# Reordering the tile body of a fused two-layer kernel on TensorE, ScalarE and VectorE

## The reference

```python
x = x + tanh(g_xattn[0]) * attention(layernorm(x), mask, ctx)         # 32 heads of 8, plus adapter attention
x = x + tanh(g_ffn[0]) * top1_experts(layernorm(x))                   # 8 experts 256x256
x = x + tanh(g_xattn[1]) * wkv(w, u, layernorm(x), ctx)               # a decaying scan over 64 steps
x = x + tanh(g_ffn[1]) * top2_experts(layernorm(x))                   # 8 gated experts, integer softmax
```

## Time and profile before

| | us |
|---|---|
| three executions | 501.67, 503.9, 503.55 |
| median | 503.55 |
| the profiled execution | 506.51 |
| its span in the trace | 504.1 |
| PE busy in the span | 464.0 (92%) |
| PE weight loads busy | 356.0 (71%) |
| DVE busy | 383.5 (76%) |
| ACT busy | 260.6 (52%) |
| POOL busy | 178.0 (35%) |

### The profile page before, as it was taken

How to read it: one execution, slowest core, us unless ns; L and a number is a source line. 1 busy time by engine, 2 the same in 40 slices (tenths; PEclk the granted TensorE clock), 3 DMA queues, 4 the chain that set the end, 5 groups by cost and what they waited for, 6 DMA issues and landing times. The chain is left out here.

```text
span 504.1 us, 10504 instructions
## 1 busy us (share of the span) xinstructions
PE 464.0 (92%) x3147; PEld 356.0 (71%) x3148; DVE 383.5 (76%) x1015; ACT 260.6 (52%) x564; POOL 178.0 (35%) x228
## 2 busy tenths in 40 slices
PE   4979899899998998999989898999999999999993
PEld 2748677777787787886866654555778788788782
DVE  5865879898889998999877889957776576575640
ACT  2755284473663752845712352525557657666641
POOL 4234212224124124231141061214455566665522
PEclk9979999899899998999999999999999999999998
DMA  7940404004004021040040589548667667668611
GB/s 225 285 93 17 74 1 85 7 23 85 16 12 86 25 53 36 21 83 18 13 85 26 197 308 383 167 138 276 237 167 248 206 208 258 187 225 235 179 22 21
DMA packets 24785, 63.37 MB, mean 126 GB/s; under 512 B 5192, under 2 KB 15312, under 8 KB 21808
## 3 DMA queue, kind: packets, MB, share of 16 engines
q1 hardware_dynamic: 19472, 56.38, 36.9%
q0 software_dynamic: 4416, 6.03, 6.5%
q10 hardware_dynamic: 864, 0.54, 0.3%
HBM read 48.79 MB, written 5.24 MB: 107 GB/s over the span
## 5 line engine op out<-in xcount | busy, mean ns | idle before, releaser
L2070 PE MATMUL bank_o<-w,hT 128*128 (+1 forms) x276 | 68.3, 389 | 2.0 <-DVE hT L1419 1.0
L1433 DVE TENSOR_TENSOR wl<-lw,wh 128x1024 fp32r<-128x1024 f32 (+1 forms) x54 | 60.9, 1129 | 1.4 <-ACT wh L652 1.4
L2070 PEld LDWEIGHTS bank_o<-w,hT 128*128 128x128 f32 (+1 forms) x276 | 48.8, 189 | 16.2 <-issue 11.5
L652 ACT ACTIVATE wh<-lw 128x1024 fp32r<-128x1024 f32 (+1 forms) x54 | 52.9, 981 | 1.9 <-DMA lw<-in_w 1.9
L1118 DVE TENSOR_REDUCE mx<-bank_s 128x8 f32<-128x512 f32 x64 | 43.0, 687 | 9.1 <-PE bank_s L1805 8.8
L502 POOL TENSOR_SCALAR rstd<-mv 128x1 f32<-128x1 f32 x32 | 7.4, 232 | 115.0 <-DVE mv L1029 115.0
L1803 PE MATMUL bank_s<-Kh,Qx 128*128 128x128 f32 x256 | 40.9, 282 | 1.4 <-DVE mx L1118 1.0
L606 POOL DMA_INDIRECT out_x<-ys,idx_out x18 | 29.0, 1609 | 36.9 <-ACT ys L929 36.1
L1803 PEld LDWEIGHTS bank_s<-Kh,Qx 128*128 128x128 f32 x256 | 35.8, 190 | 6.1 <-DVE mx L1118 3.3
L1426 DVE TENSOR_TENSOR hh<-sg,bank_s 128x256 f32<-128x256 f32 x46 | 19.0, 418 | 27.2 <-ACT sg L918 25.3
L1860 PEld LDWEIGHTS bank_o<-Vx,Pt 128*64 128x64 f32 x1024 | 32.5, 138 | 9.1 <-issue 5.8
(11 more groups left out here) (376 smaller groups left out, 1171.7 us busy)
## 6 DMA issues: line engine op xcount, KB each, us to landing
lw<-in_w SPq DMA_DIRECT2D x18, 1408.0 KB, 6.4
Q<-Qx SPq DMA_DIRECT2D x16, 512.0 KB
up<-in_w SPq DMA_DIRECT2D x5, 1408.0 KB, 8.4
w<-in_w SPq DMA_DIRECT2D x4, 1536.0 KB, 13.3
Pt<-in_WT SPq DMA_DIRECT2D x1, 1024.0 KB, 11.0
CT<-in_ctxT SPq DMA_DIRECT2D x1, 896.0 KB, 9.1
X<-in_x SPq DMA_DIRECT2D x1, 768.0 KB, 7.4
out_x<-X SPq DMA_DIRECT2D x6, 128.0 KB, 1.7
```

The costliest lines, as they stand in the source:

```text
L652: return act.activation(dst, src, ACT.Copy, scale=scale)
L1433: dve.tensor_tensor(wl[par][:, :, at:at + k], lw[par][:, :, at:at + k], wh[par][:, :, at:at + k].bitcast(F32), ALU.subtract).then_inc(w_lo, 1)
L2070: ins = pe.matmul(bo[:, 0:HID], hT[0:k, i, :], w2[0:k, bass.ts(e, 1), i, :].rearrange("p o n -> p (o n)"), start=(i == 0), stop=(i == IT - 1))
```

## The change

Five moves in the body `tile` of three engines; no instruction's operands change, and PE gets two added matmuls per tile.

- ACT: keys and values of batch 1 are evacuated directly behind `gate(t - 1)`, ahead of `evac_comb`, `evac_qT` and the first `spread`.
- DVE: `gate(u)` stands behind `wkv_inverse(w)`, not ahead of it.
- PE: `project_kv(t + 1, 1)` stands directly behind `project_kv(t + 1, 0)`; `constant_products(bo, 2)` is added ahead of `gate_logits`; the two `scores` of head group 0 stand ahead of `turn_comb`, and in their old places only `low_and_shift` is left.

```diff
--- before.py
+++ after.py
@@ -854,10 +854,10 @@
                 high_h2(t - 1)
                 evac_v(t + 1, 1 - par, 0)
                 gate(t - 1)
+                evac_v(t + 1, 1 - par, 1)
                 evac_comb(t - 1)
                 evac_qT(t + 1)
                 spread(t + 1, 1 - par, range(HG // 2))
-                evac_v(t + 1, 1 - par, 1)
                 exps(t, 0)
                 spread(t + 1, 1 - par, range(HG // 2, HG))
                 exps(t, 1)
@@ -1551,9 +1551,9 @@
                 rope_q(t + 1)
                 sum_q(t + 1)
                 shift_low(t)
-                gate(u)
                 if prev2:
                     wkv_inverse(w)
+                gate(u)
                 low_q(t + 1)
                 if prev2:
                     wkv_out(w)
@@ -2149,20 +2149,23 @@
                 output(t - 1)
                 row_scores(t, par, range(6, 8))
                 project_kv(t + 1, 0)
+                project_kv(t + 1, 1)
                 turn_h2(t - 1)
                 turn_maxima(t)
+                constant_products(bo, 2)
                 gate_logits(t - 1)
                 turn_q(t + 1)
-                project_kv(t + 1, 1)
+                scores(t, par, 0, 0, True, True)
+                scores(t, par, 0, 1, True, True)
                 turn_comb(t - 1)
                 experts0(t - 1, 0)
                 experts0(t - 1, 1)
                 if prev2:
                     turn_y(t - 2)
-                attend(t, par, 0, True, True)
+                low_and_shift(t, par, 0, 0)
                 experts0(t - 1, 2)
                 experts0(t - 1, 3)
-                attend(t, par, 1, True, True)
+                low_and_shift(t, par, 0, 1)
                 bias0(t - 1)
                 attend(t, par, 2, True, True)
                 second_half(t, par, prev2, nxt2)
```

## The result

| | kernel before | changed kernel |
|---|---|---|
| median, us | 503.64 | 518.66 |
| lowest and highest | 501.67 to 503.9 | 517.49 to 521.89 |
| the profiled execution | 506.51 | 517.49 |
| span of it | 504.1 | 515.0 |

The changed kernel is slower: ratio 1.0317, 95% interval [1.0261, 1.0373]. In a later job, beside the other kernels, it came out at 518.67 us against 503.56, ratio 1.0278 [1.0225, 1.0331] (run e11). The forecast was 514.6 us, with a range from 508.5 to 518.5.

A forecast was written before the change was run, and what follows sets the result against it. TensorE and VectorE, both nearly full and waiting on each other, bound the tile. 10.5 us for tiles 2 to 6 plus 0.6 for tile 1, clock unchanged, gave +11.1: 517.6 profiled, 514.6 median, range 508.5 to 518.5.

The forecast's parts named there:

- The chain: Tile body: reciprocal delays gate's chain and Exp, then batch 1 evacuation, scores, experts, `qs` and `low_q`; 2.1 us a tile.
- the 1.12 us from the copy to the Exp's end: Gate's chain: from the chain's copy on DVE to the Exp pair's end on ACT, 1.12 us, putting that end at 165.6.
- 2.1 us for each of the five tiles: Tiles t = 2 to 6, where the reciprocal stands ahead of the gate: each ends 2.1 us late, 10.5 in all.
- +0.6: Tile 1, which has no reciprocal: 0.6 us longer, between 0.2 and 1.2, after the four saved matmuls.
- Lowered clock: unchanged, three stretches.: Tile body: stretches partly run at 1.2 GHz stay three as before, so the clock adds nothing to the sum.
- Rival 1: Remaining three tiles also run into lowered clock behind PE's 2.5 us hole: +2.5, 517.1 us in the median; chance 0.13.
- Rival 2: PE between 160.0 and 164.7: filled holes give 4.4 us, full clock 2.4; together -6.8, 496.8 us; chance 0.05.
- Rivals 3 and 4: Tiles' idle time takes up the delay: wholly, no change, 503.6 us, chance 0.05; or half, +5, 508.6 us, chance 0.09.
- PE's before the batch 1 scores: Tile 4 sign: one PE wait of 2 to 3 us before the batch 1 scores, released by ACT's V evacuation.
- ACT's before the Exp: Tile 4 sign: ACT idle some 1.5 to 1.9 us before the gate's Exp, released by DVE.
- DVE's before `low_q`: Tile 4 sign: DVE idle 1.5 to 2 us before `low_q` (L1091), released by ACT's copy `qs`.

The follow-up runs named there:

- e11: Changed kernel as it is, measured again beside the other kernels in a later job: 518.67 us, ratio 1.0278 to the kernel before.
- e6: Changed kernel with four constant products put between the two scores, in TensorE's hole of 2 us: 512.40 us, ratio 1.0189 to the kernel before.
- e5: Kernel before with its two TensorE holes filled by constant products, three ahead of turn_h2 and one ahead of the logits: 501.87 us, ratio 0.9968.
- e7: Kernel before with second projection split around turn_h2 and turn_q, one constant product ahead of logits, batch 0 scores ahead, changed kernel's ScalarE order: 501.42 us.
- e8: Changed kernel with VectorE's order undone and batch 1 scores moved behind the first two expert pairs: 503.20 us, ratio 1.0010 to the kernel before.
- e9: e7 with the batch 1 scores also moved ahead, behind the first two expert pairs: 501.48 us, ratio 0.9959 to the kernel before.
- e4: Changed kernel with eight constant products between the two scores, 1.9 us of work in a hole of 2 us: 512.69 us, ratio 1.0176 to the kernel before.
- e10: Changed kernel, VectorE's reciprocal still ahead of the gate, only the batch 1 scores moved behind the first two expert pairs: 513.30 us, ratio 1.0192.
- e2: Kernel before with only VectorE's swap, the reciprocal ahead of the gate: 508.65 us, ratio 1.0097 to the kernel before.
- e1: Changed kernel with VectorE's order undone, the gate again ahead of the reciprocal: 507.97 us, ratio 1.0095 to the kernel before.

## Why the prediction was wrong

**The chain: right in its steps, somewhat too large.** Times less 4.39, forecast against measured: `turn_h2` 161.4, 161.41; reciprocal 162.7, 162.69; chain's copy 164.5, 164.35; end of the Exp pair 165.6, 165.26; batch 1 evacuated 166.7, 166.37; batch 1 scores 166.75, 166.43; experts 167.3, 167.03; `low_q` 168.3, 168.11; third expert pair 170.55, 170.35. By the end of the Exp pair the forecast is 0.34 us late: 0.15 at the chain's copy, and the rest because the 1.12 us from the copy to the Exp's end had ACT's V copies counted in; it took 0.91. At the third expert pair 0.20 is left of it. The full-clock tile came to 35.59 where 35.8 was said, tile 1 to 32.94 where 33.3 was said. "2.1 us for each of the five tiles" and "+0.6" for tile 1 were, at full clock, from e6 against e5 tile by tile: 1.92, 1.79, 1.94, 2.02, 1.36, and 0.26 for tile 1. Sum 9.3 instead of 11.1. Tile 6 came out furthest below; VectorE has less to do in it (27.95 us against 30.65 in tile 4), but no run shows that this is why.

**The clock: the step that failed.** "Lowered clock: unchanged, three stretches." That let the changed kernel lose to the clock only what the kernel before loses: 3.0 us in the profiled execution that the sum starts from, and about 1.9 us in the median that it ends at (503.74 less 501.87 for e5). The changed kernel lost 6.3 us of its median (518.67 in e11 less 512.40 in e6) and 6.4 us of its profiled execution: four stretches, not three, at 1.6 us each and not 1.0. So in the median this term was 4.4 us too small, while the chain's was 1.8 us too large and hid part of it. Together they make 2.6 of the 4.1 us between 514.6 and 518.66. Most of the other 1.5 us lies between e5 and e6: their medians are 10.5 us apart and their tiles 9.3. It stays open; what comes behind the tiles took between 240.7 and 242.4 us in the profiled executions of all these kernels, in no order that follows an edit.

That the two profiled executions differ by 10.98 us, where the forecast's sum was 11.1, is a coincidence: 9.3 for the chain, plus 3.4 for the clock (6.4 less 3.0), less 1.8 us outside the tiles. Of these 1.8 us, 0.6 lie ahead of them, where the execution before ran lowered once more (the page's PEclk has a 7 in its third slice) and the changed one did not, and 1.3 behind them, which no run explains.

**The rivals.** Rival 1 (*more of the clock lost*) is what happened. It was right in its mechanism, too high in its count (all six tiles, where four came) and too small in its price: +2.5, at the price of before. That price belonged to the place where the stretches fell before. Rival 2's 4.4 us for holes filled on TensorE did not exist (e7), while its clock term did (e5: 1.9 us of median; for the profiled execution 2.4 were said and 3.0 measured, since the forecast held tile 5, 34.16, against tile 4, 33.65, where tile 5 at full clock takes 33.08). Rivals 3 and 4 fell: in tile 4 `low_q` came 1.87 us later and the tile took 1.94 us more, so idle time took up nothing of the delay. DVE's busy share of a tile fell to 86%, and that of the weight loads to 71%. The Trainium skill (Perfetto Trace Analysis, Identifying the Most-Contended Engine) would have pointed to spare time on TensorE; the spare time was there (eight constants in the hole made the tile no longer than four), but it lay in waits of a chain that goes round three engines. By that reading the chain would have cost nothing; it cost 9.3 us.

**What would show it.** The waits stood where they were said, with other sizes: PE's before the batch 1 scores was 1.95 us (2 to 3 said, about 2.5 in the working), ACT's before the Exp 1.25 (1.5 to 1.9), DVE's before `low_q` 2.01 (1.5 to 2). PE's is smaller because the evacuation ended 0.33 us sooner, and because the working let the batch 0 scores end at 164.2, where the trace has 164.48 (168.87 less 4.39). None of these signs was about the clock.

Open: e8's full-clock tile of 33.99 is 0.37 above e5's. The delay of `turn_h2` by the whole second projection, 0.4 us, could explain it, and e7, which avoids it, has 33.59, but no run changed that alone, so it is not shown. Why tile 4 or tile 6 is lowered in one execution and not in another, with the same holes in it, was not tried either.

## What to carry to other kernels

Before moving a step ahead on an in-order engine, list what stands behind the instruction that waits for it on every other queue: here one reciprocal of 1.73 us, put in front of a chain with an Exp on another engine, held back an evacuation that had been ready for 3.7 us, then matmuls, then a copy, and came back to the engine it started on. Count the clock as a term of its own: read the granted clock of each profiled stretch, take lowered stretches out of both sides before comparing, and price them by the work that would fall into them. Where TensorE has to wait in front of dense work that others need, constant products in the hole can be tried first: here they cost nothing that can be measured, and in e5 they gave as much as the better order of e7 and e9.

## What the hardware showed

With four constant products in a hole of 2 us, of which 1.03 us were left (e6), the clock stayed at 2.4 GHz in all six tiles of the profiled execution, and the time was 6.3 us less; eight (e4) gave no more. With the hole open (1.95 to 2.03 us) the clock fell in four of the five tiles that have the reciprocal, in each of two profiled executions. With a hole of 1.68 to 1.75 us (e10) it fell in two of five, with one of about 1.5 us (e2) in one. The size of the hole alone does not decide it: e1, with holes of 0.73 to 0.81 us at that place, had one lowered tile, and e6, with 1.03 to 1.10 us, none. In the kernel before, it fell in three tiles of six, behind single holes of 0.8 to 0.9 and 0.36 us around a few transposes and thin matmuls, and with these filled (e5) in none. Neighbouring executions of one kernel differ by 2 to 7 us, and the time goes with the mean granted clock: of the executions of before beside e5 to e8, those at a clock of 0.991 or more took 500.5 to 503.0 us, those at 0.984 or less 503.7 to 507.3.
